# Cosine attention with the values stationary: outputs that arrive turned, row sums from additions and a product with ones

## What is computed

```python
xn = _layernorm(x, g_norm)
q = xn @ Wq
kv = xn @ Wkv
k, v = (kv[..., :DIM_HEAD], kv[..., DIM_HEAD:])
q = q.reshape(B, N, HEADS, DIM_HEAD).transpose(0, 2, 1, 3)
...
sim = jnp.einsum('bhid,bjd->bhij', q, k)
attn = jax.nn.softmax(sim.astype(jnp.float32), axis=-1).astype(sim.dtype)
out = jnp.einsum('bhij,bjd->bhid', attn, v)
out = out.transpose(0, 2, 1, 3).reshape(B, N, HEADS * DIM_HEAD)
out = out @ Wout
return _layernorm(out, g_out)
```

## Time and profile before

| | us |
|---|---|
| median of three runs | 2178.11 |
| lowest, highest | 2178.01, 2178.78 |
| the profiled execution, its own time | 2181.61 |
| its span, first to last instruction | 2179.9 |

### The profile page before, as it was taken

The page is one execution under the profiler, slowest core; times in us unless marked ns, Lnnn a source line. Parts: engine busy times, 40 slices in busy tenths (PEclk is TensorE's granted clock), DMA queues, the critical chain, the costliest instruction groups (busy, mean ns, idle before and its releaser), DMA issues. The chain is left out here.

```text
span 2179.9 us, 30021 instructions
## 1 busy us (share of the span) xinstructions
PE 1972.3 (90%) x11522; PEld 1254.8 (58%) x11522; DVE 1027.5 (47%) x2236; ACT 809.2 (37%) x1780; POOL 516.0 (24%) x617
## 2 busy tenths in 40 slices
PE   6999999999899999999999999878857899999885
PEld 4556666565566766676667656723334554545653
DVE  3555555545223232333333322288854555546444
ACT  2553535545234233323332333134313234445332
POOL 1322323223011010101111100045632143542221
PEclk9999999999999999999999999999979989999998
DMA  5000000000200000000000000020000000000001
GB/s 225 1 1 1 1 1 1 1 1 1 75 1 1 1 1 1 1 1 1 1 1 1 1 1 1 1 70 1 1 0 1 1 1 1 2 1 2 1 1 39
DMA packets 9772, 24.01 MB, mean 11 GB/s; under 512 B 2448, under 2 KB 6304, under 8 KB 8864
## 3 DMA queue, kind: packets, MB, share of 16 engines
q1 hardware_dynamic: 8336, 18.92, 2.3%
q10 hardware_dynamic: 1296, 3.18, 0.4%
HBM read 20.00 MB, written 2.10 MB: 10 GB/s over the span
## 5 line engine op out<-in xcount | busy, mean ns | idle before, releaser
L1486 PEld LDWEIGHTS cos_ps<-cos_vx,cos_probs 128*128 128x128 f32 x2048 | 238.7, 191 | 33.6 <-issue 28.7
L1486 PE MATMUL cos_ps<-cos_vx,cos_probs 128*128 128x129 f32 x2048 | 239.8, 275 | 4.2 <-DVE cos_on L1171 4.2
L1477 PE MATMUL cos_ps<-lead_room,cos_kT 128*128 128x512 f32 x512 | 232.4, 598 | 6.8 <-PEq L50 6.1
L1359 ACT ACTIVATE cos_probs<-cos_ps 128x512 f32<-128x512 f32 x256 | 150.9, 597 | 172.5 <-PE cos_ps L1477 171.5
L671 ACT ACTIVATE probs<-sc,nmax 128x512 f32<-128x512 f32 (+3 forms) x256 | 132.3, 524 | 169.2 <-DVE nmax L525 167.1
L1270 POOL TENSOR_TENSOR cos_qrs<-cos_qse,neg_half 128x4 f32<-128x4 f32 x59 | 59.4, 1007 | 507.4 <-DVE cos_qse L1153 507.4
L780 PE MATMUL sc<-kT,qT 128*128 128x512 f32 (+3 forms) x512 | 172.6, 459 | 3.9 <-DVE probsT L537 2.5
L1477 PEld LDWEIGHTS cos_ps<-lead_room,cos_kT 128*128 128x128 f32 x512 | 95.2, 192 | 107.0 <-issue 104.9
L2882 DVE TENSOR_REDUCE cos_wq<-tail_ps 128x2 f32<-128x1024 f32 (+3 forms) x128 | 101.7, 823 | 83.3 <-PE tail_ps L3122 82.2
L1151 DVE TENSOR_REDUCE cos_qss<-cos_qsq 128x4 f32<-128x512 f32 x59 | 40.5, 686 | 202.0 <-ACT cos_qsq L1338 202.0
L752 PE MATMUL pq<-xnT,wap 128*128 128x512 f32 x256 | 125.6, 613 | 4.3 <-DVE swp L517 3.9
(11 more groups left out here) (486 smaller groups left out, 3452.5 us busy)
## 6 DMA issues: line engine op xcount, KB each, us to landing
onT<-in_mla_wqT SPq DMA_DIRECT2D x1, 2048.0 KB, 9.3
lead_room<-in_mla_wo SPq DMA_DIRECT2D x1, 2048.0 KB, 20.6
cos_wq<-in_cos_wq SPq DMA_DIRECT2D x1, 2048.0 KB, 25.6
cos_wout<-in_cos_wout SPq DMA_DIRECT2D x1, 2048.0 KB, 7.4
out<-x SPq DMA_DIRECT2D x4, 512.0 KB, 2.9
x<-in_x SPq DMA_DIRECT2D x1, 1536.0 KB, 14.7
wq_pe<-in_mla_wq_pe ACTq DMA_DIRECT2D x1, 1024.0 KB, 14.3
x<-in_x SPq DMA_DIRECT2D x1, 512.0 KB, 4.4
```

The lines of the kernel that those rows point to most:

```text
L1359: act.activation(probs[:, n % 2, kj, :], ps[:, kj, :], ACT.Exp).then_inc(s["e_done"], 1)
L1477: pe.matmul(ps[:, kj, :], kT[:, b % 2, kj * P:(kj + 1) * P], qT[:, hq % 2, h % 4, :], start=True, stop=True).then_inc(s["s_ready"], 1)
L1486: last = pe.matmul(po[:, qi // 2, qi % 2, :], probs[:, n % 2, kj, qi * P:(qi + 1) * P], vx[:, b % 2, kj, :], start=(kj == 0), stop=(kj == ...
```

## The change

The cosine stage computes the same, in another arrangement.

- `attend` has the values stationary and the probabilities moving: four products of 512 columns into bank 4. The result has the 128 value columns down the partitions and the 512 queries along the row, so it needs no turning. `vx` loses its column of ones, and a head's output goes straight into `onT`, now a buffer for all 16 heads.
- The row sums are made apart. `sum_tiles` (DVE) adds the four tiles of probabilities in three additions. `lengths` (PE, new, ahead of the next head's scores) multiplies each quarter of the sum by a 128x32 block of ones; each quarter of the queries goes to its own 32 partitions of half of bank 5, which holds 128 columns. `invert_lengths` (DVE) takes the reciprocal of this 128x128 block.
- SP takes four rows of the inverse (one of each 32 partitions) to a row of 512 in DRAM, waits for that to land, and loads it back into all 128 partitions of `rb`. Both DMAs are issued once a head.
- `normalise` is one multiplication of bank 4 by `rb`, and waits for that DMA too.
- At the end of a batch `turn_outputs` and both `copy_outputs` are gone. `project_outputs` waits once, for the last head's output.

```diff
@@ the plan @@
         for h in range(COS_H):
+            take(("lengths", b, h), (5,), ("l_done",))
             if h + 1 < COS_H:
                 scores(b, h + 1)
...
-            take(("attend", b, h), (4, 5), ("o_done", "o_done"))
+            take(("attend", b, h), (4,), ("o_done",))
...
@@ SP @@
+                for n in range(B * COS_H):
+                    sp.wait_ge(s["l_done"], n + 1)
+                    if n >= 2:
+                        sp.wait_ge(s["o_done"], n - 1)
+                    sp.dma_start(row[n % 2, :].rearrange("(i c) -> i c", c=P), rl[0:P:COS_QUARTER, n % 2, :])\
+                      .then_inc(s["row_written"], 16)
+                    sp.wait_ge(s["row_written"], 16 * (n + 1))
+                    sp.dma_start(rb[:, n % 2, :], row[n % 2, :].unsqueeze(0).to_broadcast([P, S]))\
+                      .then_inc(s[COS_SPREAD[n % 2]], 16)
...
@@ DVE @@
+                def sum_tiles(b, h):
+
+                    n = head(b, h)
+                    dve.wait_ge(s["e_done"], TI * n + 2)
+                    dve.tensor_tensor(sums[:, :], probs[:, n % 2, 0, :], probs[:, n % 2, 1, :], ALU.add)
+                    dve.wait_ge(s["e_done"], TI * n + 4)
+                    dve.tensor_tensor(sums2[:, :], probs[:, n % 2, 2, :], probs[:, n % 2, 3, :], ALU.add)
+                    dve.drain()
+                    dve.tensor_tensor(sums[:, :], sums[:, :], sums2[:, :], ALU.add).then_inc(s["sum_ready"], 1)
+
+                def invert_lengths(b, h):
+                    n = head(b, h)
+                    dve.wait_ge(s["l_ready"], n + 1)
+                    dve.reciprocal(rl[:, n % 2, :], ps[:, 5, (n % 2) * P:(n % 2 + 1) * P]).then_inc(s["l_done"], 1)
...
-                    dve.reciprocal(rl[:, n % 2, :].rearrange("p (a q) -> p a q", a=2), po[:, :, :, COS_D])
-                    dve.drain()
-                    dve.tensor_tensor(on[:, :, h, :].rearrange("p (a q) c -> p a q c", a=2), po[:, :, :, 0:COS_D],
-                                      rl[:, n % 2, :].rearrange("p (a q) -> p a q", a=2).unsqueeze(3)
-                                      .to_broadcast([P, 2, 2, COS_D]), ALU.mult).then_inc(s["o_done"], 1)
...
+                    dve.wait_ge(s[COS_SPREAD[n % 2]], 16 * (n // 2 + 1))
+                    dve.tensor_tensor(onT[:, h, :], ps[:, 4, :], rb[:, n % 2, :], ALU.mult).then_inc(s["o_done"], 1)
...
                 for b in range(B):
+                    sum_tiles(b, 0)
                     for h in range(COS_H):
+                        invert_lengths(b, h)
+                        if h + 1 < COS_H:
+                            sum_tiles(b, h + 1)
                         if cos_unit(b, h) is not None:
                             sum_queries(b, cos_unit(b, h))
                             scale_queries(b, cos_unit(b, h))
...
@@ PE @@
+                def lengths(b, h):
+
+                    n = head(b, h)
+                    free(("lengths", b, h))
+                    pe.wait_ge(s["sum_ready"], n + 1)
+                    for i in range(TI):
+                        last = pe.matmul(ps[COS_QUARTER * i:COS_QUARTER * (i + 1), 5, (n % 2) * P:(n % 2 + 1) * P], ones[:, :],
+                                         sums[:, i * P:(i + 1) * P], start=True, stop=True)
+                    last.then_inc(s["l_ready"], 1)
+
...
-                    for qi in range(TI):
-                        for kj in range(TI):
-                            last = pe.matmul(po[:, qi // 2, qi % 2, :], probs[:, n % 2, kj, qi * P:(qi + 1) * P],
-                                             vx[:, b % 2, kj, :], start=(kj == 0), stop=(kj == TI - 1))
+                    for kj in range(TI):
+                        last = pe.matmul(ps[:, 4, :], vx[:, b % 2, kj, :], probs[:, n % 2, kj, :],
+                                         start=(kj == 0), stop=(kj == TI - 1))
                     last.then_inc(s["o_ready"], 1)
...
+                        pe.wait_ge(s["o_done"], head(b, COS_H))
+                    for a in range(8 * half, 8 * half + 8):
+                        last = pe.matmul(y[i], onT[:, a, i * P:(i + 1) * P], wout[:, a, :],
+                                         start=(a == 0), stop=(a + 1 == COS_H))
...
                     for n in range(2 * TI):
-                        turn_outputs(b, n)
-                        if n > 0:
-                            project_outputs(b, n - 1)
-                            if more:
-                                fill(("turn", "q", b + 1, n - 1))
                         if more:
                             project(b + 1, n)
-                    project_outputs(b, 2 * TI - 1)
+                        project_outputs(b, n)
+                        if more and n > 0:
+                            fill(("turn", "q", b + 1, n - 1))
```

79 lines of the change are left out of this document (30 added, 49 removed).

## The result

| | before | after |
|---|---|---|
| median, us (runs) | 2178.06 (4) | 2211.99 (4) |
| lowest, highest | 2177.26, 2178.78 | 2210.73, 2212.58 |
| ratio to before | | 1.0155, 95% interval 1.0137 to 1.0173 |
| profiled execution's span | 2179.9 | 2210.6 |

The change costs 33.9 us, where 14.6 were forecast: the sign was right, the size less than half, and the time lies at the very top of the range. A second measurement beside other runs gave 1.0161 (1.0139 to 1.0183).

A forecast was written before the change was run, and what follows sets the result against it. PE bounds the stage, busy 787.71 of 829 us. 1.7 + 8.8 + 6.5 + 2.7 + 18.5 + 7.2 + 8.4 + 0.7 - 6.3 - 33.6 = +14.6 on 2178.1 gives 2192.7 us, range 2178 to 2212.

The forecast's parts named there:

- Part 1: Inside the heads: attend 0.14 less, `lengths` 0.27 more; +1.7 in 14 plain heads, +8.8 in 35 with a unit.
- Rival (b): In `lengths`, the array's quarters don't overlap in so short a burst: +33, 2225 us; chance 0.08.
- Part 2: DVE's reciprocal (0.94 us) and the DMA pair: covered in most heads, +6.5 us at heads 9 and 10.
- C: Time from the reciprocal's end to the landing of the spread inverses: 4.5 us, bounds 3.8 and 6.0.
- Part 3: Batch ends: +8.4 for batches 1 and 2, +0.7 batch 0, -6.3 batch 3; three boundaries -11.2 each, -33.6 us.
- Rival (g): At the boundary a half stays at 7.27 us, set by the queries' chain: +33.6, 2226 us; chance 0.03.
- Part 4: Batch starts: `lengths` of head 0 waits for DVE's sum, +18.5; lower clock, +7.2; stage's start, +2.7 us.
- (c): Clock stays at 1.00 through gaps at batch starts and ends: +3.8, 2181.9 us, no difference; chance 0.09.
- (e): (c) and (d) together: 2170 us, faster; chance 0.04.
- (a): DMA pair is slow, C = 6.0, about 10 us per us of C at batch ends: +15, 2208; chance 0.17.
- (d): DMA pair lands in C = 3.4 or less, batch ends give 12 back: +2.5, 2180.6 us; chance 0.06.
- (f): DVE's reciprocal costs 0.28 us: +4.6, 2182.7 us; chance 0.03.

The follow-up runs named there:

- e1: Changed kernel with the four row-sum products of each head issued twice, same result; 2226.72 us, ratio to before 1.0211.
- e7: Changed kernel plus products nobody reads on PE ahead of each batch's first row sums, in the time it only waited; 2201.46 us, ratio to before 1.0090.
- e6: Changed kernel, but the load spreading the inverses takes the previous head's row, not waiting for its own head's store; 2203.11 us, ratio to before 1.0112.
- e5: Changed kernel, three orders moved: first-head `lengths` behind next scores, reciprocals from head 12 ahead of side work, next batch's first sums earlier; 2175.51 us, ratio to before 0.9981.

## Why the prediction was wrong

The sum was worked out for the program; the stage shows +33.1 in the profile, 18.5 more than the sum. By stretches of the stage, in us over before:

| stretch | forecast | measured |
|---|---|---|
| from the stage's start to the first projection | +2.7 | +5.0 |
| heads up to the attend of head 12 (Part 1 and heads 9, 10) | +17.0 | +28.1 |
| four ends of batches | +2.8 | +5.6 |
| three boundaries | -33.6 | -32.8 |
| three batch starts, with the clock | +25.7 | +26.8 |

By its steps:

- **Part 1, `lengths` at 0.27: the step that failed.** It cost 0.55. In the 49 heads of Part 1 that is 0.28 to 0.30 each, about 14 us of the 18.5. The 34 ns a record of the earlier trace rows were near (27 measured), on the dear side. But the row is of long trains beside their like. PE's timeline of before, where one of them stands:

```profile
1629.42 1.92 PE L2447 MATMUL tail_ps<-cos_wout,wsp_cw 128*32 128x512 f32 x16 [1.27 <-ACT cos_wout L2361]
1631.14 1.08 PE L2437 MATMUL tail_ps<-ident,wsp_inv 128*32 128x128 f32 x32
```

  It is 32 records behind another group with 32-column weights, so it shows the records and not the turn from the whole array. I took the price of a record for the price of a group. The estimate of 0.36 from the Trainium skill's 2.38 times (TensorE: Matmul & The Clock Gate, Part 3) is what the group shows from its start to the next; e1's second set at 0.21 says that this agreement is by accident, since 0.14 of it is the turn. Rival (b) named the right term with the wrong reason: the quarters do overlap.
- Part 1, attend 3.44 and the 5.44 chain of a unit: right (3.43, 5.44).
- Part 2, reciprocal 0.94 and C = 4.5: right (0.95, 4.7), though the split was not (store 1.6, load 3.1 instead of 2.0 and 2.5). The estimate of 0.26 for the reciprocal from the Trainium skill (VectorE: DVE Perf Modes, the TRN2 errata) does not fit this trace's 0.95; the slope of the earlier trace rows does. Head 9's turning in batch 0 waited 2.1, forecast 2.7; over all batches what was forecast at +6.5 for heads 9 and 10 came to some 3.5, which hid part of the miss on `lengths`.
- Part 3: boundary -11.2 each: right (-11.1, -10.9, -10.9). End of batch 1 +4.2: +4.7; batch 2 +4.9; batch 0 +0.7: +1.2; batch 3 -6.3: -5.2. The ends are together 2.8 us short; `lengths` stands in those heads too, at 0.28 more than I had. Rival (g) fell with the halves of 5.61.
- Part 4, batch starts +8.6 each with the clock: right (+8.4, +9.1, +9.3; waits 4.86 and 4.87), 1.1 short in all. The stage's start was +2.7 and came to +5.0 (from first scores to projection 14.38 against 9.33): I had the wait (2.18) but not the lower clock behind it. That is 2.3 more; e7 took 1.7 of it away.
- Rivals (c), (e): the clock did fall, with 0.57 to 0.65 in the windows behind the gaps. (a), (d), (f): C and the reciprocal were where the sum had them, and e6 shows about the ten us for each us of C that (a) counted on.

The heads are 11.1 short (14.2 for `lengths`, less the 3 too many for heads 9 and 10), the ends 2.8, the start 2.3, the batch starts 1.1 and the boundaries 0.8: 18.1 of the 18.5. That 33.9 was measured between the medians and 33.1 stands in one trace of each is partly chance, since the second trace of after has 36.2.

What the runs add to the forecast's reasoning is the order. I had costed the waits at the batch starts and ends as belonging to the change. They belonged to where four groups, the reciprocals from head 12 on and the first additions of a batch stand. In e5 a batch start, from the last product with `wout` to the second head, costs 2.0 us more than before instead of 8.4 to 9.3, the ends of batches 0 to 2 are 0.8 to 1.2 shorter than before, and the change then just pays for itself.

## What to carry to other kernels

Price a new small group of products from a place where its neighbours are of the other shape, from the start of the group ahead to the start of the one behind the next, and not from a train of its like. Before you count a wait as the price of a change, ask which queue the waited-for step stands in and whether it could stand elsewhere: here three moves of order were worth as much as the change lost. And when PE is made faster, look for rings of VectorE and DMA that it has no part in, since they set how much of the gain arrives.
